# Cross-attention on one core: the short key block's projections, the row-sum steps and VectorE's running sum moved to other chunks

## What is computed

```python
Q = x @ W_Q; K = ctx @ W_K; V = ctx @ W_V      # split into 16 heads of 64
scores = Q K^T / 8;  attn = softmax(scores);  context = attn V
out = context @ W_O + x
out = (out - mean) / sqrt(var + 1e-5)          # over the last axis
```

## Time and profile before

| | before |
|---|---|
| median of 3 runs | 1605.02 us (1604.69 to 1605.4) |
| the profiled execution, its own time | 1603.05 us |
| its span | 1601.3 us |
| PE busy | 1589.1 us (99%) |
| DVE busy | 1348.2 us (84%) |
| ACT busy | 928.8 us (58%) |
| POOL busy | 300.0 us (19%) |
| mean granted clock of PE | 0.999 |

### The profile page before, as it was taken

The page is one execution under the profiler, slowest core; times in us unless marked ns, Lnnn a source line. Parts: engine busy times, 40 slices in busy tenths (PEclk is TensorE's granted clock), DMA queues, the critical chain, the costliest instruction groups (busy, mean ns, idle before and its releaser), DMA issues.

```text
span 1601.3 us, 43898 instructions
## 1 busy us (share of the span) xinstructions
PE 1589.1 (99%) x19164; PEld 827.4 (52%) x19164; DVE 1348.2 (84%) x1397; ACT 928.8 (58%) x1080; POOL 300.0 (19%) x313
## 2 busy tenths in 40 slices
PE   9999999999999999999999999999999999999998
PEld 4576666434664346643566435563365533665335
DVE  7898798887988879887798878988789887888877
ACT  4445566556665556655566566565666555655553
POOL 4842022120121202201021011220112102121100
PEclk9999999999999999999999999999999999999999
DMA  6321011000110001100011000110011000110000
GB/s 214 94 76 31 11 32 59 12 31 12 48 51 2 30 22 49 41 2 31 21 49 41 2 30 21 59 32 2 30 32 51 30 9 23 32 59 22 9 1 15
DMA packets 31618, 56.68 MB, mean 35 GB/s; under 512 B 7120, under 2 KB 13392, under 8 KB 31424
## 3 DMA queue, kind: packets, MB, share of 16 engines
q1 hardware_dynamic: 31136, 53.51, 10.8%
q10 hardware_dynamic: 288, 0.33, 0.1%
HBM read 48.02 MB, written 5.30 MB: 33 GB/s over the span
## 4 chain that ended last, share of the span: by engine, by line
PE 97%; DVE 2%; issue 0%; ACT 0%; POOL 0%; DVEq 0%; ACTq 0%
PE o_ps L674 43%; PE s_ps L657 42%; PE w_ps L723 5%; PE w_ps L740 2%; PE w_ps L754 1%; PE w_ps L759 1%; DVE v_all L1067 1%; PE w_ps L775 1%; PE w_ps L776 1%; PE w_ps L755 0%; PE w_ps L772 0%; PE w_ps L761 0%; DVE sums L1110 0%; PE s_ps L852 0%; DVE inv_sum L1220 0%
## 5 line engine op out<-in xcount | busy, mean ns | idle before, releaser
L971 ACT ACTIVATE probs<-s_ps 128x1024 f32<-128x1024 f32 x801 | 819.8, 1024 | 625.7 <-PE s_ps L657 613.2
L1110 DVE TENSOR_TENSOR sums<-sums,probs 128x1024 f32<-128x1024 f32 x785 | 988.1, 1259 | 123.8 <-ACT probs L971 88.5
L674 PE MATMUL o_ps<-probs,v_all 64*64 64x512 f32 x6408 | 881.7, 589 | 0.0
L657 PE MATMUL s_ps<-q_sb,k_all 64*64 64x512 f32 x6408 | 876.9, 589 | 0.0
L674 PEld LDWEIGHTS o_ps<-probs,v_all 64*64 64x64 f32 x6408 | 315.5, 133 | 315.5 <-issue 257.5
L657 PEld LDWEIGHTS s_ps<-q_sb,k_all 64*64 64x64 f32 x6408 | 306.7, 133 | 292.2 <-issue 239.9
L610 POOL TENSOR_TENSOR crossed<-crossed 128x128 f32<-128x128 f32 x84 | 41.8, 498 | 744.0 <-ACT crossed L989 744.0
L1067 DVE TENSOR_REDUCE v_all<-w_ps 128x512 f32<-128x1024 f32 (+2 forms) x103 | 121.6, 1181 | 36.1 <-PE w_ps L723 34.5
L723 PEld LDWEIGHTS w_ps<-wv_sb,ctx_all 64*64 64x64 f32 x3176 | 108.1, 133 | 45.3 <-issue 19.0
L723 PE MATMUL w_ps<-wv_sb,ctx_all 64*64 64x128 f32 x3176 | 115.2, 270 | 0.2 <-DVE y L1135 0.2
L613 POOL TENSOR_TENSOR crossed<-crossed 128x128 f32<-128x128 f32 x84 | 98.7, 1175 | 6.6
(11 more groups left out here) (115 smaller groups left out, 666.1 us busy)
## 6 DMA issues: line engine op xcount, KB each, us to landing
c_forms<-forms_dram SPq DMA_DIRECT2D x84, 384.0 KB, 3.1
forms_dram<-c_forms SPq DMA_DIRECT2D x12, 384.0 KB, 2.5
inv_sum<-inv_dram SPq DMA_DIRECT2D x30, 128.0 KB, 2.9
attn<-in_ctxT SPq DMA_DIRECT2D x24, 128.0 KB, 2.9
ctx_all<-in_ctxT SPq DMA_DIRECT2D x11, 256.0 KB, 6.1
quad_rows<-quad_sums SPq DMA_DIRECT2D x60, 4.0 KB, 1.8
c_forms<-in_ctxT SPq DMA_DIRECT2D x12, 64.0 KB, 2.4
x_sb<-in_x SPq DMA_DIRECT2D x1, 512.0 KB, 9.4
```

The source lines that it names most:

```text
L657: last = nc.tensor.matmul(s_ps[part(half), u % 2, head * QH:(head + 1) * QH], k_all[part(head), c * P + half * DH:c * P + (half + 1) * DH] ...
L674: last = nc.tensor.matmul(o_ps[part(head), rows, :], v_all[part(rows), key_chunk(t, c, head), part(head)], probs[part(rows), u % RING, hea ...
L971: nc.scalar.activation(probs[:, u % RING, :], s_ps[:, u % 2, :], ACT.Exp, scale=SCALE).then_inc(probs_ready, 1)
L1110: nc.vector.tensor_tensor(out=sums[0:rows, t % 2, :], in0=sums[0:rows, t % 2, :], in1=probs[0:rows, u % RING, :], op=ALU.add).then_inc(sum ...
```

## The change

Short K block from chunk 40 to 42 and short V block from 43 to 45 (for the pairs after the first); the transpose of the sums from chunk 2 to 4, the fold from 4 to 8, the inverses from 9 to 12; POOL's norm and weight forms four places later in its queue; SP loads the forms of blocks 5 and 6 between the fold and the inverses, where it loaded that of block 5 alone; `SUMS_AHEAD` goes from 1 to 2, so that in DVE's queue the sum of chunk u + 2 stands behind the take of iteration u.

```diff
-    TURN_STEP, FOLD_STEP, INV_STEP = 2, 4, 9
+    TURN_STEP, FOLD_STEP, INV_STEP = 4, 8, 12
...
-    SUMS_AHEAD = 1
+    SUMS_AHEAD = 2
...
-    NORM_STEP, W_FORMS_STEP = 13, 20
+    NORM_STEP, W_FORMS_STEP = 17, 24
+    LAST_BLOCK_STEPS = (42, 45)
...
             at = c - 2 if t == 0 else c
+            if pair > 0 and c >= LAST_BLOCK_STEPS[0] - 2:
+                return ("kv"[LAST_BLOCK_STEPS.index(c)], pair, FULL_BLOCKS) if c in LAST_BLOCK_STEPS else None
...
                 if h == 0:
-                    load_forms(pair, 5)
+                    for b in range(5, 7):
+                        load_forms(pair, b)
                 sp.wait_ge(inv_lines_ready, t + 1)
...
                 if h == 0:
-                    for b in range(6, FULL_BLOCKS):
+                    for b in range(7, FULL_BLOCKS):
                         load_forms(pair, b)
```

## The result

The changed kernel takes 1607.15 us (median of 22 runs, 1605.12 to 1610.29), the kernel before 1604.29 (22 runs, 1603.36 to 1605.4). The ratio is 1.002, its 95% interval 1.0014 to 1.0026. So the change makes the kernel about 2.9 us slower; forecast was 0.4 us faster. The time lies in the range, and on the wrong side of no change.

What follows compares the result with a forecast made beforehand. PE was taken to bound the kernel (97% of the span), so only late matmul starts count. Terms -6.0 - 2.8 + 4.9 + 3.2 + 0.3 = -0.4 us against 1603.05; with the median 1.97 higher, forecast 1604.5 us, range 1599.5 to 1611.

Steps and rivals of the forecast that it cites:

- short K at 42: Even passes, chunk 40: PE's 0.85 us wait for DVE to take the short K goes in seven passes, -6.0 us.
- row-sum steps, with the sum in even passes: Even passes: moved transpose, fold and inverses let r(4), V(7), V(11) start nearer on time, -0.4 a pass, -2.8 us.
- block 5's load late: Even passes, chunk 12: load issued behind the later fold makes r(12) wait, 0.7 in seven passes, +4.9 us.
- sum in odd passes: Chunks 40 to 42: sum in front of k's take delays V's take and r(42), 0.45 in seven passes, +3.2 us.
- start: Start of the kernel, once: two sums instead of one stand before the first K block's take, +0.3 us.
- rival B: Steady blocks of even passes: k's take pushes V, some 49 blocks at 0.4, +20 us, 1624; chance 0.06, mild form included.
- its mild form: Chunk 4 alone: the transpose meets POOL's add of r(4) and runs 0.4 late, +2.8 us, 1607.3; chance half of 0.06.
- Rival D: Even passes: the short K's wait only moves, another wait takes the 0.85 us, 1610.5 us; chance 0.02.
- Rival A: Gains stand, waits for block 5's load and in odd passes don't appear: 1596.5 us; chance 0.1 in full, 0.12 in part.
- Rival C: Even passes: block 5 lands in 3.5 us, and V(3), V(7), V(11) lose 0.25 each: 1610.6 us; chance 0.15.

Runs made afterwards that it cites:

- exp. 5: Kernel before with only the short K block moved to chunk 42 and the short V block to 45: 1597.78 us, ratio 0.9965.
- exp. 1: Changed kernel with SP issuing block 5's load right behind block 4's, ahead of the wait for the fold: 1598.72 us, ratio to the kernel before 0.9964.
- experiment 12: Changed kernel with 32 one-column matmuls (128 PE instructions) added at the start, shifting PE's instruction fetches: 1619.1 us, ratio to the kernel before 1.0091.
- experiment 3: Changed kernel with `add_left` moved from chunk 40 to 32 in odd passes: 1602.47 us, ratio to the kernel before 0.999.
- experiments 1 and 8: Changed kernel with block 5's load ahead of the fold's wait; 8 also has the sum one chunk ahead: 1598.72 and 1596.22 us.
- experiment 7: Changed kernel with block 5's load ahead of the fold's wait and `add_left` at chunk 32 in odd passes: 1594.09 us, ratio to the kernel before 0.9937.
- experiment 2: Changed kernel with block 6's load held back until block 5's has landed: 1607.7 us, ratio to the kernel before 1.002.
- experiment 6: Kernel before with only DVE's sum moved to two chunks ahead: 1614.34 us, ratio 1.0065.
- experiment 4: Changed kernel with DVE's sum put back to one chunk ahead: 1604.19 us, ratio to the kernel before 0.9999.

## Why the prediction was wrong

Each term against what it measured, in us of the whole kernel:

| term | forecast | measured |
|---|---|---|
| short K at 42 | -6.0 | -5.9 in the windows, -6.3 in runs (exp. 5) |
| row-sum steps, with the sum in even passes | -2.8 | -3.0 in the windows (exp. 1 against 5) |
| block 5's load late | +4.9 | +8.0 in the windows, +8.4 in runs (exp. 1) |
| sum in odd passes | +3.2 | +3.7 in the windows |
| start | +0.3 | +0.35 at V(1) |
| sum | -0.4 | +3.1; runs +2.9 |

**The step that failed** is the load of block 5: "It is 0.6 late and costs 0.7, in seven passes: +4.9." The mechanism and the usual size were right: 0.68 to 0.83 in four passes. The size was wrong in the other three. In passes 6 and 12 the landing took 4.4 and 4.2 and not 3.1, since a fetch of instructions falls into the load (experiment 12), and that is 1.3 and 1.1 on top of the usual cost. In pass 10 a fetch falls among the small DMAs instead, the load goes out 2.89 behind the fold instead of 2.53, and 0.3 is added. Together that is 2.7 of the 3.1 missing; the rest is that the usual case costs 0.76 and not 0.70, seven times. The sign hung on this term, as the others sum to -5.3 by forecast and to -4.9 measured.

I had the slow landing in my rows, 4.8 us, and left it out of the bounds as one that "had the broadcast loads in front of it". That was argued, not looked up, and it was wrong. The slow one is block 6's load of pass 4. Block 6's load has the same loads in front of it in all seven even passes, and the other six land in 3.2 to 3.6 us; the slow one has a packet of q8 1.86 us behind its issue. Block 5's own landings in the kernel before were 4.24 and 4.73 in passes 6 and 12, each with a packet 0.97 or 0.98 behind its issue, where seven us of cover hid them. A maximum that the new place would no longer hide belonged into the sum for the passes that have it. With those two landings in it the same working gives 4.9 + 1.1 + 1.6 = +7.6 for the load, a total of +2.3 and the right side.

**The rest of the steps.** The short K starts without idle time, and r(4) follows its product on time: right. The load goes out 2.53 behind the fold, PE waits for it in seven passes: right, but the longest is 1.8, where near 0.6 was said. Odd passes 91.48 for 91.4: right, and experiment 3 shows the row on DVE that causes it. V in steady blocks never waits: nothing of rival B, in either form. What spoke against it held: with the steps at their new place the sum in front of k's take costs 0.05 a pass in experiments 1 and 8. That its mild form gave 1607.3, next to the 1607.15 measured, is chance: r(4) is on time. Rival D didn't happen (experiment 5). Rival A, that the new waits don't appear, is what experiment 7 brings about by its edits: A gave 1596.5, and 1594.09 came out. Of the 2.4 between them 0.8 are odd passes, each 0.11 below that of the kernel before, since the edit also removes the 0.26 lost at r(42), of which 0.1 had been made up at chunk 44; 0.4 are even passes, 9.2 less in all where A had 8.8; and 1.0 is the kernel before, 1604.07 beside experiment 7 and 1605.02 in the working. Rival C had the right direction, but a wrong mechanism, a later landing in every pass: experiment 2 shows that the load behind costs nothing, and the added lateness is in three passes. That the range held the time is owed to C's price, not to its cause. Even passes were to be 0.5 shorter each; because of the load they are 0.13 shorter on average.

**What I would say otherwise.** I costed the sum and the row-sum steps one by one, and in their combination that was near enough. Alone they would have been wrong: experiment 6 came out 6 us above what I expected, since I moved the sum past the takes and not past the transposes and inverses.

**What stays open.** The profiled executions differ by 5.4 us and the medians by 2.9. Of the 5.4, even and odd passes give -0.9 and +3.7; the first scores are 1.24 later and pass 0 is 0.93 longer, of which 0.35 is V(1); 0.46 lies in the last pass and the tail. The executions of after also differ more among themselves, by 5.2 us against 2.0 before; a part of that goes with the clock, as the last section shows. The start varies between executions (first scores at 6.9 to 8.3 us in kernels that don't differ there), and no experiment was made on it.

## What to carry to other kernels

When a load's issue is moved behind other work, its slack has to cover the slowest landing that this load already has somewhere in the trace, pass by pass, not the median: cover that hid a slow landing goes away together with the cover of the others. A load whose buffer is free should not stand in a queue behind a wait for another engine; taking it out in front was worth 8.4 us here, at no price. And instructions that run back to back on an engine are one thing: an insert in front of them is paid in full at their end, and is cured at any member of the row (`add_left` at 32).

## What the runs showed of the hardware

**Fetching instructions delays loads.** The DMA queue table of the page after has

```profile
q8 instruction: 153, 2.51, 0.7%
```

153 packets of 16 KB, about one per 256 of PE's and its weight loads' 38,328 instructions. A packet that starts 1.0 to 1.5 us behind a 384 KB load's issue made it land in 4.2 to 4.7 us instead of 2.9 to 3.3 (block 5's load in after, experiments 2 and 12), and adding 128 instructions moved the effect to other passes. In all fourteen traces together 41 loads of `c_forms` have a packet of q8 0.8 to 1.6 us behind their issue, and land in 3.8 to 4.9 us; the median of all such loads is 3.1. The Trainium skill ("Runtime: NRT & Kernel Launch", instruction fetch mechanics) has the sequencer fill its instruction memory in blocks of 16 KiB, 256 instructions, over a DMA queue of its own, at a cost that is mostly hidden. The block size agrees with the 153 packets. No wait of PE is put down to its own fetch here, but it stood still for a load that the fetch had made later.

**Waits of PE of about 2 us were followed by a lower clock, but not all of them.** In experiment 12, pass 4, r(12) waits for 2.02 us. PE, and the windows before, behind and after that:

```profile
450.07 0.29 PE L758 MATMUL w_ps<-c_forms,w_forms 64*64 64x128 f32 x1 [2.02 <-DMA c_forms<-forms_dram]
```

```profile
448.00:450.90 2.90, 0.88 (x24) 0.67 (x24) 2.73 (x5) 0.47 (x2) 0.00 (x0) 1.00 0.31 119
450.90:454.40 3.50, 3.50 (x24) 1.34 (x20) 1.42 (x4) 2.19 (x4) 0.91 (x2) 0.52 0.12 41
454.40:458.00 3.60, 3.60 (x56) 2.75 (x52) 2.54 (x5) 1.72 (x2) 0.00 (x0) 0.99 0.37 113
```

The granted clock is full while PE mostly stands still, half (1.2 of 2.4 GHz) in the 3.5 us behind it, and full again. At 0.52 these 3.5 us lose 3.5 x 0.48 = 1.7 us of work. Pass 4 takes 107.18, 4.0 more than the 103.20 of experiment 1, so the idle time accounts for 2.3 and the clock for the rest. Pass 10, with a wait of 1.95 us, takes 107.11 and has a mean clock of 0.98 too. In after the longest wait, 1.79 us, was followed by no such fall, and neither was the longest of all, 2.28 us in experiment 4: pass 6 there takes 105.72 at full clock. So the length of the wait alone doesn't decide it, and what else does isn't shown.

Nor is it the same in every execution. The profiled one of experiment 12 took 1621.82 us at a mean clock of 0.997, the other three 1618.2 to 1619.35 at 0.999. Of the 22 executions of after, seven have a mean clock of 0.997 or 0.998 and a median of 1608.9 us, the other fifteen 0.999 or more and 1606.9. In the kernels with block 5's load in time, before included, 2 of 94 executions are below 0.999. So a part of what the late load costs in runs goes with the clock, and the windows of the profiled execution, all at full clock, don't show it; that the waits cause the falls was not tested by itself.
